# Reordering the sixteen causal attention units of a two-layer transformer kernel, with a light unit of each query chunk first

## What is computed

```python
x = x + L0_attn(layernorm(x))   # 16 heads of 8, rotary, causal softmax, S = 2048
x = x + L0_ffn(layernorm(x))
x = x + L1_attn(layernorm(x))   # 16 heads of 8, rotary, not causal
x = x + L1_ffn(layernorm(x))    # top 2 of 8 experts
```

```python
scores = einsum('bhsd,bhtd->bhst', q, k) / sqrt(8)
scores = where(causal, scores, -inf)
attn   = softmax(scores, axis=-1)
out    = einsum('bhst,bhtd->bhsd', attn, v)
```

## Time and profile before

| what | value |
|---|---|
| median of three executions | 1794.83 us (1789.95 to 1795.75) |
| span of the profiled execution, first to last instruction | 1802.3 us |
| that execution against the median | 7.5 us longer |
| mean granted TensorE clock, share of full speed | 0.927 |
| TensorE matmul busy, whole span | 1667.7 us (93%) |
| VectorE busy | 1157.5 us (64%) |
| ScalarE busy | 1115.9 us (62%) |
| causal attention, from the first instruction of its loops to the last copy out | 53.0 to 512.65 us of the span |

### The profile page before, as it was taken

One profiled execution on the slowest core, in us unless ns is written; L12 is line 12 of the kernel. 1 busy time (PEld: TensorE's weight loads), 2 busy tenths in 40 slices (PEclk: granted clock), 3 DMA queues, 4 the chain that ended last, 5 costly groups with the idle time before them and its releaser, 6 DMA issues. The chain is left out here.

```text
span 1802.3 us, 31760 instructions
## 1 busy us (share of the span) xinstructions
PE 1667.7 (93%) x12488; PEld 768.9 (43%) x12488; DVE 1157.5 (64%) x1566; ACT 1115.9 (62%) x1996; POOL 116.3 (6%) x206
## 2 busy tenths in 40 slices
PE   6889899999989997878999999999999998699999
PEld 3444343343344443323333333333333334477776
DVE  7677989997141112598999999999999834311111
ACT  3547587788852221315888888888888885244343
POOL 3121110100000000200000000000000000000000
PEclk9569999999999997756999999999999999599999
DMA  3100000000000001000000000000000000000000
GB/s 104 65 1 1 1 2 1 1 2 2 1 1 0 0 0 55 0 1 1 1 2 1 1 1 2 1 1 1 1 1 2 1 1 1 24 13 24 12 23 23
DMA packets 16772, 17.13 MB, mean 10 GB/s; under 512 B 2995, under 2 KB 13696, under 8 KB 16128
## 3 DMA queue, kind: packets, MB, share of 16 engines
q1 hardware_dynamic: 16639, 15.32, 2.7%
HBM read 14.26 MB, written 1.05 MB: 8 GB/s over the span
## 5 line engine op out<-in xcount | busy, mean ns | idle before, releaser
L612 DVE TENSOR_REDUCE maxp<-banks 128x2 f32<-128x1024 f32 (+3 forms) x800 | 942.9, 1200 | 137.1 <-PE banks L452 71.1
L593 ACT ACTIVATE probs<-banks 128x512 f32<-128x512 f32 x1568 | 843.1, 596 | 203.9 <-PE banks L478 157.0
L497 PE MATMUL banks<-probs,V 128*9 128x256 f32 (+3 forms) x6016 | 487.3, 398 | 3.7 <-POOL probs L556 3.0
L478 PE MATMUL banks<-Q,K 64*128 64x512 f32 (+3 forms) x1664 | 435.0, 484 | 8.4 <-ACT probs L593 5.0
L452 PE MATMUL banks<-K,Q 64*128 64x512 f32 (+3 forms) x1664 | 375.8, 434 | 35.0 <-DVE maxp L612 34.4
L478 PEld LDWEIGHTS banks<-Q,K 64*128 64x128 f32 x1664 | 180.0, 188 | 363.9 <-ACT probs L593 287.0
L452 PEld LDWEIGHTS banks<-K,Q 64*128 64x128 f32 x1664 | 177.7, 198 | 85.6 <-DVE maxp L612 70.3
L497 PEld LDWEIGHTS banks<-probs,V 128*9 128x9 f32 x6016 | 91.4, 89 | 252.5 <-ACT probs L593 190.8
L1004 DVE SCALAR_TENSOR_TENSOR x<-banks,wts,x 128x128 f32<-128x128 f32 x128 | 36.1, 345 | 196.4 <-PE banks L967 196.4
L992 ACT ACTIVATE work<-banks,eb 128x512 f32<-128x512 f32 x128 | 86.3, 688 | 104.7 <-PE banks L958 102.6
L967 PEld LDWEIGHTS banks<-work 128*128 128x128 f32 x1024 | 118.1, 192 | 11.5 <-issue 11.5
(11 more groups left out here) (127 smaller groups left out, 855.4 us busy)
## 6 DMA issues: line engine op xcount, KB each, us to landing
tables<-in_tables SPq DMA_DIRECT2D x2, 2048.0 KB, 10.3
work<-in_ew SPq DMA_DIRECT2D x16, 256.0 KB, 2.9
flex<-in_h SPq DMA_DIRECT2D x2, 1024.0 KB, 8.4
x<-in_x SPq DMA_DIRECT2D x4, 256.0 KB, 3.9
out<-x SPq DMA_DIRECT2D x4, 256.0 KB, 2.3
cst<-in_consts SPq DMA_DIRECT2D x1, 865.0 KB, 6.0
flex<-in_w SPq DMA_DIRECT2D x3, 256.0 KB, 3.0
flex<-in_w_qk SPq DMA_DIRECT2D x1, 256.0 KB, 6.1
```

What stands on the lines that cost most here:

```text
L478: mm = pe.matmul(ebank(e)[:, at:at + CW - low], k.K[rows, 2 * g + block, kt * P:(kt + 1) * P], k.Q[rows, n % 3, block, low:CW], start=True ...
L497: mm = pe.matmul(acc[32 * j:32 * j + HD + 1, low + a:low + z], k.V9[:, kt, g * HG + j, :], k.probs[:, tile, at + a:at + z], start=(s == 0) ...
L593: act.activation(k.probs[:, number % 8, :], ebank(e), ACT.Exp, scale=scale).then_inc(e_done, 1)
L612: dve.tensor_reduce(dst, src, AX.X, ALU.max).then_inc(m_done, 1)
```

## The change

It gives `units` another order for the causal layer, and it copies the accumulator of unit n to the slot of its chunk and group, where before n was that slot. The new order is (0,0), (1,0), (2,0), (3,0), (3,1), (3,2), (3,3), (2,1), (2,2), (2,3), (1,1), (1,2), (1,3), (0,1), (0,2), (0,3). Everything else in the phase is worked out from `units`: bank numbers, semaphore counts and `plan`. Layer 1 keeps its order.

```diff
@@ -309,6 +309,9 @@
     causal = layer == 0
     scale = SCALE0 if causal else SCALE1
     units = [(c, g) for c in range(C) for g in range(G)]
+    if causal:
+        units = ([(c, 0) for c in range(C)] + [(C - 1, g) for g in range(1, G)]
+                 + [(c, g) for c in reversed(range(C - 1)) for g in range(1, G)])
     NU = len(units)
 
     def reductions(n):
@@ -640,7 +643,7 @@
 
             def take_acc(n):
                 dve.wait_ge(pv_done, group_base[n + 1])
-                dve.tensor_copy(k.outT(n), acc).then_inc(acc_free, 1)
+                dve.tensor_copy(k.outT(units[n][0] * G + units[n][1]), acc).then_inc(acc_free, 1)
 
             def segment(n):
                 acc_after = sum(len(slot) for slot in plan(n + 1)[:2]) if 0 <= n < NU - 1 else 0
```

## The result

The changed kernel takes 1801.39 us (median of 20 executions, 1794.37 to 1805.27), the kernel before 1792.45 us in the same comparison (20 executions, 1789.11 to 1804.06). The ratio is 1.0034, with a 95% interval of 1.0020 to 1.0048: slower, by little more than the 0.3% that I had named as what a measurement can tell from no change. The medians lie 8.9 us apart; the ratio, which is not the quotient of the medians, stands for 6.1 us. I had forecast 1795 us and the three signs nearly alike.

What follows compares the result with a forecast made beforehand. VectorE's reductions pace units carrying a heavier chunk, TensorE and ScalarE the other units; -0.3 us in the phase and 0.8 at the output phase made +0.5, added to the 1794.83 us median: about 1795 us, range 1782 to 1807.

Steps and rivals of the forecast that it cites:

- the three signs: Whole kernel against the one before: faster 0.31, same 0.40, slower 0.29.
- the second rival: TensorE's clock drops in unit 1 and units from 11 on, together +13 us, 1808 us; chance 0.27.
- the sum: Causal phase: units 435.8 us plus 23.5 ahead of them, 459.3 against 459.65, so -0.3 us.
- Each reduction left out is worth 0.10 us: Causal units that VectorE doesn't pace: each missing reduction saves 0.10 us, as in units 5 and 6.
- their base: Chunk-3 units: unit 4 stands between old units 12 and 13 at 38.3 us; units 5, 6 at 37.8, 37.7.
- The light units: Units 10 to 15, chunks 1 and 0 at the end: 20.3, 19.7, 19.7, 13.2, 10.5 and 7.0 us.
- the first rival: The tail's units 8, 9, 11, 12 give back more, unit 0 too: -18 us, 1777, likelier half, 1786; chance 0.30.
- The front: Ahead of the loop +7.3 us; then unit 0 at 37.0, unit 1 at 33.5, unit 2 at 34.8 us.
- The term at nothing: Units behind the front: the sum included no cost for drops of TensorE's clock there.

Runs made afterwards that it cites:

- the second profile: The kernel before, unchanged, profiled and timed again: ratio 0.9988, median 1790.59 us.
- the run above: Changed kernel with one reduction beside each half until used up, then none, in units with fewer reductions than halves: ratio 1.0033 against the kernel before.
- the two profiles of the changed kernel: The changed kernel's first profile and one of it run again unchanged, the latter at ratio 1.0031 against the kernel before, median 1799.60 us.
- The repeated starts: Changed kernel with a second pass of the maxima's score matmuls beside the first two halves of causal units from 5 on: ratios 1.0026 and 1.0027.
- the fuller starts: Changed kernel with two reductions beside each causal unit's first half and one more beside the second, where urgent ones suffice: ratio 1.0039 against the kernel before.

## Why the prediction came out as it did

**The range held, the sign was missed narrowly.** 1801.4 lies between 1782 and 1807, though outside the forecast's own 1788 to 1800. The forecast was a change of nothing; 0.34% slower lies on the side of the second rival, which had stood for +13 us. That the sum came near the measured windows was luck in part, as the terms below show.

**The step that failed most is the reference of the sum.** "459.3, against 459.65" compared 16 terms with one execution, and that one carried about 6 us of clock drops inside the phase. I took units 1 and 15 at 13.23 and 35.93 as their price; free of drops they are 10.20 and 33.33. Against the 453.0 us of the second profile my own sum of 459.3 would say +6.3 us, or a ratio of 1.0035. That this meets the measured 1.0034 is chance: the sum carries the same inflated price of chunk 0, and 453.0 is the phase of a single execution at the lower end of the times. I had noted that the profiled execution was 7.5 us above the median, and added the difference to the median without asking which rows carried the 7.5. The hint stood in the rows, where the clock was 0.67 and 0.74 in the two lightest units and 0.90 in the last, which I took as given.

**"Each reduction left out is worth 0.10 us" was too much in the long units, and their base too low.** Units 5 and 6 with 24 and 23 reductions took 39.4 and, without a drop, 38.9, as unit 3 did with all (39.2); units 8 and 9 took 29.0 and 29.2 against the 29.46 of the earlier trace rows. That is 0.7 us for 24 missing reductions, 0.03 each. In the chunk-1 units 11 and 12, where half of the halves are free, it was 0.15 (18.4 and 18.7 for unit 10's 19.4). The larger part of the miss in units 4 to 6 is their base, 38.3 for 39.6 in unit 4: I averaged with the old unit 13, whose window of 37.37 is short only by where it is cut. From the scores of its own second half (399.32) to those of unit 14's (438.33) the old unit 13 takes 39.0 us, as unit 4 does. But the last values of a unit, and VectorE's copy behind them, come after the next unit's second half, and in unit 14 that half has no queries to build and no reduction beside it. The last values of the old units 12 and 13:

```profile
401.94 0.62 PE L497 MATMUL banks<-probs,V 128*9 128x256 f32 x8
...
439.34 0.62 PE L497 MATMUL banks<-probs,V 128*9 128x256 f32 x8
```

They start 2.62 us after the scores at 399.32, but 1.01 us after those at 438.33. Why single reductions left out bring so little can be read off TensorE. Unit 3 of the changed kernel's first profile, a reduction beside each half, only the scores (L481) shown; start and length are the first numbers:

```profile
194.62 0.51 PE L481 MATMUL banks<-Q,K 64*128 64x512 f32 x2
...
195.84 0.51 PE L481 MATMUL banks<-Q,K 64*128 64x512 f32 x2
...
197.07 0.51 PE L481 MATMUL banks<-Q,K 64*128 64x512 f32 x2
```

The scores start 1.22 and 1.23 us apart. Unit 6 of the same profile, its clock back at 1.00 from 305 us on, where the half at 313.59 has no reduction (L455 maxima, L596 exponentials):

```profile
313.59 0.50 PE L481 MATMUL banks<-Q,K 64*128 64x512 f32 x2
...
314.19 2.06 ACT L596 ACTIVATE probs<-banks 128x512 f32<-128x512 f32 x4 [0.16 <-PE banks L481]
...
314.57 0.76 PE L481 MATMUL banks<-Q,K 64*128 64x512 f32 x2
...
314.91 0.66 PE L455 MATMUL banks<-K,Q 64*128 64x512 f32 x2
...
316.05 0.50 PE L481 MATMUL banks<-Q,K 64*128 64x512 f32 x2
...
316.64 2.30 ACT L596 ACTIVATE probs<-banks 128x512 f32<-128x512 f32 x4 [0.39 <-PE banks L481]
...
318.50 0.50 PE L481 MATMUL banks<-Q,K 64*128 64x512 f32 x2
```

The next scores start 0.98 us later, 0.25 early. But ScalarE is still at its four exponentials from 314.19 to 316.25, the scores' second bank comes free late (0.76 us long instead of 0.50), and maxima and values stand behind it on TensorE. The following half starts at 316.05, 1.48 us on, and ScalarE has idled 0.39 us for it. The four halves from 313.59 to 318.50 take 4.91 us, 1.23 each, as with reductions. A single free half gains nothing; free halves in a row run faster, as in units 14 and 15 of before and at 1.11 us in the run above. Together these terms were 4.6 us too low (units 4, 5, 6, 8, 9 without drops 176.0, predicted 171.4), 1.7 of it by the 0.10.

**The light units were too dear.** Units 10 to 15 free of drops took 78.6 us (the lower of the two profiles for each), predicted 90.4. Most of it is chunk 0, priced at the 13.23 of a unit at 0.74. That is the first rival's side, 12 us; with the drops' 6.7 and the 4.6 above it cancels to nearly nothing, which is luck, and is why the sum looked right.

**The front was right.** Ahead of the loop +7.9 us (24.1 for 16.15; predicted +7.3), unit 0 35.6 and 38.6 around the predicted 37.0, unit 1 33.5 and 34.0, unit 2 exact. Its mechanism holds as far as tested: VectorE was busy for 28.4 us of unit 0 in both profiles, and the clock moves the rest, as I had taken it (38.6 at 0.50, 35.0 at 0.65). How far full clock alone would bring it is open.

**The term at nothing: the clock behind the front.** The second rival had the mechanism, but the wrong places. The sum gave the changed order no drops of its own; the rival put them in unit 1 and from 11 on. They came at starts of units from 5 to 14, 6.7 us in each profile and 2.6 us each in a long unit. Less these drops the phase is 451.7 and 455.2 us in the two profiles of the changed kernel, around the 453.0 of the old one's better profile; with them it is 5.4 and 8.9 us over it. Against the old one's other profile it is 1.2 us under and 2.4 over, so profiles alone don't give the 6 us of the ratio; the clocks of all executions do. The Trainium skill (TensorE: Matmul & The Clock Gate, Part 1) says that the array's slow clock is its default and that activity releases it. The trace agrees in part: the low stretches stand at starts of units, with 0.64 from 295 to 300 us and 0.51 from 370 to 375 in the first profile of the changed kernel and ScalarE busy for 3.2 and 2.3 of the 5 us, but the profile's row has TensorE busy for all 5 of both.

**What stays open.** The repeated starts took 6.7 us of drops out of the phase and cost 2.9, so 3.8 us should come back. By mean times it was 3.4 (1800.1 to 1796.7), but from executions at other times; against the kernel before, timed beside each, the ratio went only from 1.0031 and 1.0034 to 1.0026 and 1.0027, within the intervals. That the loss goes with the clock is shown by the executions; that the clock leads and the time follows, and in which units of the unprofiled executions it fell, is not. Behind the phase spans went from 1281 to 1290 us whatever the order. Nor is it shown why the fuller starts kept their drops.

## What to carry to other kernels

Before pricing a change from one profile, see where its own time stands among the runs, and search the rows for what that execution had and others may not: here the reference moved by 6.6 us, as much as the change. Where each execution's clock is on record, compare two kernels at the same clock. Leaving the second engine's work out of single turns gained nothing here, since the pair of engines that paces the loop has its own ring of buffers; count the loop's period with and without the work, over several turns. Reordering here moved a surplus about, and at the same clock the total stayed within a microsecond. And a test that adds work to hold the clock needs the price of that work, or it answers neither question.

## What the runs showed of the hardware that was not expected

- Over 152 executions of the two kernels the time followed the mean granted clock, 1.3 us for each 0.001, and at the same clock the two orders differed by less than 1 us.
- The same program's causal phase took 459.6 and 453.0 us, and 458.4 and 461.9 after the change, and nearly every difference sits in windows where the granted clock was below 1.00. A drop in a unit of chunk 2 or 3 cost 2.6 us in these profiles.
- Three passes of the maxima's matmuls at full clock hold TensorE for 0.96 us, one pass at the lower level for 0.79. They brought unit 0 from 38.64 us (0.50) and 35.65 (0.60) to 34.34 (1.00), and units 2 and 3 of the old order from 40.1 to 39.1 together.
- Doing score matmuls twice beside two halves per unit held the clock at 1.00 through eleven units in both profiles, for up to 0.6 us a unit; the same amount of work merely moved forward did not.
